# Three instructions' places in a four-layer graph kernel: a normalisation, a check of weights and a set of columns

## The reference

```python
h = relu(layernorm(x))
# layer 0: w = row softmax of adj^T where adj != 0 (adj is 0 or 1: a mean over neighbours)
x += BN(w^T @ BN(w @ h @ kernel_1 + bias_1) @ kernel_2 + bias_2)   # BN over all graphs and nodes
# layer 1 (A): Wh = h @ W^T; s, t = Wh @ a_src, Wh @ a_dst
x += softmax(where(adj, leaky_relu(s_i + t_j), -inf)) @ Wh
# layer 2 (B): e = leaky_relu(h_i * a_k . h_j), k picked by adj; adj == 1 is the only kind here
x += softmax(where(adj == 1, e, -9e15)) @ h
# layer 3 (C): as layer 1 with its own W and a, then elu
x += elu(softmax(where(adj > 0, leaky_relu(s1_i + s2_j), -9e15)) @ Wh)
```

## Time and profile before

| | us |
|---|---|
| median of three runs | 1505.93 |
| profiled execution | 1506.49 |
| its span (first to last instruction) | 1504.7 |
| TensorE busy | 1375.7 (91%) |
| VectorE busy | 1177.1 (78%) |
| ScalarE busy | 818.6 (54%) |
| GpSimd busy | 384.2 (26%) |

### The profile page before, as it was taken

One profiled execution on the slowest core, in us unless ns is written; L12 is line 12 of the kernel. 1 busy time (PEld: TensorE's weight loads), 2 busy tenths in 40 slices (PEclk: granted clock), 3 DMA queues, 4 the chain that ended last, 5 costly groups with the idle time before them and its releaser, 6 DMA issues.

```text
span 1504.7 us, 33033 instructions
## 1 busy us (share of the span) xinstructions
PE 1375.7 (91%) x12642; PEld 1238.7 (82%) x12642; DVE 1177.1 (78%) x3400; ACT 818.6 (54%) x1843; POOL 384.2 (26%) x337
## 2 busy tenths in 40 slices
PE   5899998899946888999999999999999999999886
PEld 5899997555536778999999999989999889999785
DVE  5788885788746668888888898888988889887565
ACT  4788885122243564565746656556565565654621
POOL 6343430000010304314133141331423314223020
PEclk9999998899968989999999999999999999999998
DMA  9999993566612213132331432314323134132111
GB/s 206 224 226 231 223 217 130 183 241 239 208 39 76 71 41 94 50 106 83 94 93 50 113 100 71 95 51 109 106 64 99 52 104 113 44 86 56 30 43 44
DMA packets 111840, 169.36 MB, mean 113 GB/s; under 512 B 9808, under 2 KB 61760, under 8 KB 109632
## 3 DMA queue, kind: packets, MB, share of 16 engines
q1 hardware_dynamic: 87264, 125.20, 28.9%
q0 software_dynamic: 19584, 33.56, 12.3%
q10 hardware_dynamic: 4832, 8.45, 1.5%
HBM read 158.74 MB, written 42.00 MB: 133 GB/s over the span
## 4 chain that ended last, share of the span: by engine, by line
PE 48%; DVE 11%; DVEq 4%; ACT 3%; POOL 2%; issue 2%; ACTq 0%
PE ps L1703 31%; PE ps L1662 3%; PE ps L1685 2%; PE ps L1716 2%; PE ps L1630 2%; DVE wts_C L1010 2%; PE ps L1674 2%; PE ps L1676 2%; PE ps L1675 2%; POOL wts_B L923 1%; DVEq L1033 1%; DVE xC L1087 1%; DVE st_B L945 1%; DVE xB L1040 1%; PE ps L1639 1%
## 5 line engine op out<-in xcount | busy, mean ns | idle before, releaser
L1703 PE MATMUL ps<-hV,wts_B 128*128 128x129 f32 x2048 | 252.4, 279 | 13.0 <-POOL wts_B L923 5.2
L923 POOL TENSOR_TENSOR wts_B<-wts_B,off 128x1024 f32<-128x1024 f32 (+7 forms) x128 | 177.8, 1413 | 323.0 <-PE ps L1685 323.0
L1703 PEld LDWEIGHTS ps<-hV,wts_B 128*128 128x128 f32 x2048 | 241.3, 194 | 17.4 <-POOL wts_B L923 7.3
L1703 PE MATMUL ps<-hP_A,wts_A 128*128 128x129 f32 x1920 | 230.9, 275 | 1.1 <-ACT xB L1429 0.7
L1703 PEld LDWEIGHTS ps<-hP_A,wts_A 128*128 128x128 f32 x1920 | 221.5, 191 | 3.8 <-DVE hP_C L994 2.9
L1703 PE MATMUL ps<-hP_C,wts_C 128*128 128x129 f32 x1920 | 220.1, 274 | 0.0
L1703 PEld LDWEIGHTS ps<-hP_C,wts_C 128*128 128x128 f32 x1920 | 217.4, 191 | 0.5
L1010 DVE SCALAR_TENSOR_TENSOR wts_A<-row_A,least_A,ring_A 128x1024 f32<-128x1024 f32 x128 | 161.0, 1274 | 11.4 <-ACT row_A L1384 7.9
L1010 DVE SCALAR_TENSOR_TENSOR wts_C<-row_C,least_C,ring_C 128x1024 f32<-128x1024 f32 x120 | 166.7, 1401 | 0.0
L316 ACT ACTIVATE maskT<-ps 128x1024 fp8e4<-128x1024 bf16 x128 | 131.2, 1025 | 45.4 <-PE ps L360 33.0
L372 PE MATMUL ps<-x,adj_b 128*128 128x129 f16 x896 | 121.3, 224 | 20.9 <-DVE x L237 13.9
(11 more groups left out here) (243 smaller groups left out, 2713.7 us busy)
## 6 DMA issues: line engine op xcount, KB each, us to landing
adj_b<-in_adj POOLq DMA_DIRECT2D x120, 256.0 KB, 10.4
maskT_scratch<-maskT SPq DMA_DIRECT2D x16, 1024.0 KB, 6.8
ring_A<-maskT_scratch SPq DMA_DIRECT2D x64, 256.0 KB, 3.1
off<-maskT_scratch SPq DMA_DIRECT2D x32, 512.0 KB, 6.6
ring_C<-maskT_scratch SPq DMA_DIRECT2D x64, 256.0 KB, 3.4
xa<-in_x SPq DMA_DIRECT2D x16, 512.0 KB, 16.3
whT_b<-whT_scratch SPq DMA_DIRECT2D x16, 512.0 KB, 4.8
pTf_scratch<-pT_b SPq DMA_DIRECT2D x16, 512.0 KB, 2.9
```

Of the source, the lines that this page charges most:

```text
L923: pool.tensor_tensor(w, w, off_fp8[:, k, k * P:N], ALU.mult).then_inc(S["B", "up"], 1)
L1703: last = nc.tensor.matmul(Q_SLOTS[c // 2 % 2][:, c % 2, 0:PW], wts[y][:, j, c * P:c * P + P], src[:, j, :], start=(j == 0), stop=(j == T - 1))
```

## The change

Three edits, none of which adds or removes an instruction.

1. In the first stage, shifts, normed, high and low of the next graph each move ahead by one tile: shifts from c = 3 to c = 2, low from c = 6 to c = 5. Statistics and moments stay at c = 0 and 1.
2. In the second stage, later_weights_dve moves behind graph(1) on VectorE, and later_weights_pe behind the first product on TensorE.
3. In the last stage, in steps with C at work, columns("A", i + 1) moves ahead of weights("C", i - 2, 4). exponents stays behind it. This is so in steps 2 to 14, 13 of them.

```diff
--- before.py
+++ after.py
@@ -261,13 +261,13 @@
                                 stats(b + 1, c)
                             if more and c == 1:
                                 moments(b + 1)
-                            if more and c == 3:
+                            if more and c == 2:
                                 shifts(b + 1)
-                            if more and 3 <= c < 5:
-                                normed(b + 1, c - 3)
+                            if more and 2 <= c < 4:
+                                normed(b + 1, c - 2)
+                            if more and c == 4:
+                                high(b + 1)
                             if more and c == 5:
-                                high(b + 1)
-                            if more and c == 6:
                                 low(b + 1)
                         rest(b, T - 1)
                         nc.vector.tensor_copy(rdeg_all[:, b * T:b * T + T], rdg[:, :])
@@ -644,8 +644,8 @@
 
                     first_norm_dve(dve)
                     graph(0, 0, True)
+                    graph(1, 1, True)
                     later_weights_dve(dve)
-                    graph(1, 1, True)
                     for k in range(0, B // 2 - 1):
                         for par in range(2):
                             stats(k * 2 + par, par)
@@ -726,9 +726,9 @@
                     first_norm_pe(pe)
                     pe.wait_ge(m_kept, 1)
                     rows(0, 0, 0, True)
-                    later_weights_pe(pe)
                     rows(1, 1, 0, False)
                     product(0, 0, True)
+                    later_weights_pe(pe)
                     rows(2, 0, 1, False)
                     product(1, 1, True)
                     rows(3, 1, 1, False)
@@ -1257,10 +1257,11 @@
                         if AA:
                             stats("B", newB, 1)
                             moments("B")
+                        if nextA and i != 0:
+                            columns("A", i + 1)
                         if CA:
                             weights("C", i - 2, 4)
                         if nextA and i != 0:
-                            columns("A", i + 1)
                             exponents("A", i + 1)
                         if AA:
                             shifts("B", i)
```

## The result

| | before | after |
|---|---|---|
| median, 7 runs each, one chip | 1506.73 us | 1515.8 us |
| lowest and highest | 1505.83, 1508.25 | 1512.51, 1519.18 |
| ratio, 95% interval | 1 | 1.0061 (1.005 to 1.0073) |
| profiled execution, its span | 1506.49, 1504.7 | 1515.19, 1513.4 |
| first stage, until the last rest (L251) starts | 249.32 | 269.33 |

The program is 0.6% slower, at the time that was predicted (1515.3). Two single runs of the experiments stand apart: one of the twelve of part 2 alone took 1516.61 us at a mean granted clock of 0.916 (the others 0.965 to 0.967) and is in its ratio, one of the six of parts 2 and 3 took 6394.82 us and is not.

A forecast was written before the change was run, and what follows sets the result against it. It took three nearly full engines to bound the first stage and TensorE's issue the last. 18.8 - 3.6 - 5.8 = +9.4 on a span of 1504.7 gave 1515.9 profiled, 1515.3 as median; whole range 1506 to 1526.

The forecast's parts named there:

- Part 1, +18.8: First stage: normalisation a tile earlier lengthens the batch period from 13.95 to 15.44 us; +18.8 us, bounds 13 to 23.
- the stall at tile 5: First stage, TensorE: tile 5's products wait something over 1 us for tile 2's rest, roughly replacing 0.93 us per batch.
- the dearer one: First stage: tile 6's tail falls behind low, so ScalarE's divide of tile 6 starts 1.82 us later.
- Part 2, -3.6: Second stage: the weights' check behind the first product lets rows(1) start 4.1 us earlier; -3.6 us, bounds -4.7 to -2.5.
- I let rows(1) and the product last as long as they do now: Second stage, TensorE: assumed unchanged durations for rows(1) and the first product, within the -3.6 us.
- Part 3, -5.8: Last stage: columns ahead of weights C 4 bring sf_B 0.53 us earlier in 11 steps; -5.8 us, bounds -6.8 to +4.8.
- The choice that L1010, begun 0.22 behind the power's start, leaves it alone: Last stage: GpSimd's power taken as free, 1.64 us instead of 2.60 to 2.63, with rs_B at 898.39.
- Power blocked later: Rival, last stage: the moved L1010 still stretches GpSimd's power, costing +4.8 us; total 1525.9 us, chance 0.19.
- Row_A takes the whole gain: Rival, last stage: sf_B stays where it is, so the columns' move gains 0; total 1521.1 us, chance 0.12.
- Exchange of waits in the first stage: Rival: TensorE's 0.93 us wait per batch becomes 1.2 to 1.3 at tile 5, +3.6 us; total 1500.1, chance 0.07.
- Full gain: Rival: the first stage's 13.9 us of TensorE waits for x go; total 1482.6 us, chance 0.02.
- The sum: Whole program: 18.8 - 3.6 - 5.8 = +9.4 us, giving 1515.3 us; chance 0.57.

The follow-up runs named there:

- part 2 alone: The kernel before with only the weights' check moved behind the first product in the second stage; ratio 0.9987 to the kernel before.
- parts 2 and 3: The kernel before with the check and the columns moved but the first stage's normalisation left where it was; ratio 0.9927 to the kernel before.
- after, rest 2 ahead: The kernel after with VectorE's rest of tile 2 put ahead of shifts, into the wait for the power; ratio 1.0035 to the kernel before.
- part 1 alone: The kernel before with only the first stage's normalisation moved a tile earlier; ratio 1.0129 to the kernel before.
- part 3 alone: The kernel before with only the columns moved ahead of weights C 4 in the last stage; ratio 0.996 to the kernel before.
- the loop without ScalarE's waits: The kernel before with check and columns moved, and ScalarE's store of the first half moved behind the next batch's first divide; ratio 0.9932 to the kernel before.

## Why the prediction was right, step by step

- **Part 1, +18.8: measured +19.4.** Its rows came as worked out: sf_a bound to the power with 1.17 us idle (forecast: 1.1 or more), low 5.13 behind sf_a, divide 6 at 6.75 (forecast 68.09 - 61.34 = 6.75), the last rest at 9.51 (9.49), 5.97 (5.95) from it to sf_a, period 15.45 in the regular batches and 15.53 in the mean (15.44).
- **One step of part 1 was wrong though the sum was right.** I wrote that the stall at tile 5 "would roughly replace the 0.93 us" and that tile 6 was "the dearer one". It is, but by 0.25 us only: with tile 6's tail back ahead of low the loop is still 15.21. The stall makes TensorE's transposes late for ScalarE, which has no slack left until the last rest, and so costs 1.25 us a batch by itself. I followed the late tile on TensorE only, not to the engine behind it.
- **Part 2, -3.6: -3.4 and some -5 in the runs (-2.0 with the run of 1516.61 us), -4.6 in the rows.** From the first row (L622) to the second people copy are 27.82 us before and 23.23 after. The mis-sized term is "I let rows(1) and the product last as long as they do now". From the end of L630 to the second L622 are 7.96 us before and 3.14 after, 4.8 less where I had 4.1. The granted clock tells why (last column but two). Windows of the kernel before, then of the kernel after:

```profile
270.00:274.00 4.00, 0.23 (x1) 0.24 (x2) 3.68 (x11) 1.04 (x1) 0.00 (x0) 0.50 0.54 229
274.00:278.00 4.00, 4.00 (x19) 3.86 (x20) 1.37 (x9) 0.00 (x0) 0.00 (x0) 0.50 0.00 0
```

```profile
288.00:289.00 1.00, 0.16 (x1) 0.19 (x2) 0.90 (x2) 0.27 (x1) 0.00 (x0) 1.00 1.06 438
289.00:290.00 1.00, 1.00 (x9) 1.00 (x9) 1.00 (x2) 0.78 (x1) 0.00 (x0) 0.86 0.99 418
290.00:291.00 1.00, 1.00 (x7) 1.00 (x7) 1.00 (x2) 0.00 (x0) 0.00 (x0) 0.50 0.88 369
```

  Before, TensorE had idled 7.29 us and the clock was 0.50, the 1.2 GHz level, while rows(1) ran: 3.76 us. After, it had idled 3.72; the clock was still full (2.4 GHz) when rows(1) began at 288.84 and was at 0.50 from 290 on: 2.95 us. The shorter wait alone doesn't give this. All four kernels with the wait of 7.29 us have 3.76, but the ten with part 2, all with a wait of 3.72 or 3.73, have anything from 2.02 at a clock of 1.00 (part 2 alone) to 3.75 at 0.50 (after, rest 2 ahead):

```profile
271.25 2.02 PE L710 MATMUL ps<-k,whT_b 128*128 128x128 f32 x16 [3.73 <-DVE row L630]
```

```profile
285.83 3.75 PE L712 MATMUL ps<-k,whT_b 128*128 128x128 f32 x16 [3.73 <-DVE row L632]
```

  The other 1.4 us of the stage (17.19 from the last rest to the first row, after 15.82) lie ahead of the edit, and 1.0 of them is the clock too: the 16 matmuls of rows(0) took 3.00 us at a granted clock of 0.64 before and 2.04 at 1.00 after. No part of the change brings it: from the last rest to the first row are 16.01 us with part 1 alone, 16.28 with part 2 alone, 17.28 with part 3 alone and 15.83 with parts 2 and 3. What decides the clock here stays open, as do the other 0.4 us.
- **Part 3, -5.8: measured -6.0.** Worked out per step 0.53, in the trace 0.54. The choice that L1010, begun 0.22 behind the power's start, leaves it alone was the dearest one (it decided on the rival of a power blocked later, 0.19), and it was right: 1.64 us. The rule of the Trainium skill (GPSIMD Engine Reference, Key points) that the two engines contend when VectorE reads two SBUF inputs holds here only when L1010 is running at the power's start: the power takes 2.60 to 2.63 us with L1010 begun 0.17 ahead, though they overlap for 1.11 us, and 1.64 with it begun 0.22 or 0.56 behind, though all of its 1.28 us lie over the power. L1010 itself takes 1.28 either way. And not every VectorE instruction does it: at the start of the power of 569.29, which takes 1.64, one of 0.82 us with an input in PSUM was running:

```profile
569.11 0.82 DVE L1025 TENSOR_TENSOR wts_B<-ps,off 128x640 f32<-128x640 f32 x1
```

- **The rivals.** Power blocked later: out; all 13 powers rs_B from 600.59 to 1339.40 take 1.64 us. The 14th, at 1398.23, in a step without columns, where L1010 begins 0.16 ahead of it, still takes 2.60. Row_A takes the whole gain: out; it starts 2.46 after sf_B, as before, and moved with it. Exchange of waits in the first stage (1500.1): out, the last rest moved by 1.84, not by less than 0.5. Full gain: out.
- **The sum** hit within 0.5 us, partly by luck: part 1 was 0.6 under its measure, part 2 a microsecond short on the other side. By stages the profiled executions differ by +20.0, -6.0 and -5.4 where the terms were +18.8, -3.6 and -5.8; about 1.8 of the -6.0 is a clock that no term held (1.0 at rows(0), 0.8 at rows(1)).

## What to carry to other kernels

Moving a step that waits for another engine ahead is worth nothing unless what it waits for moves too: it turns the work that used to cover the wait into work behind the block. Follow each displaced instruction to the engine that consumes it, and on through that engine's queue; where three engines are nearly full, several closed chains can be nearly as long (here 15.45 and 15.20 us), and an experiment that removes one shows only the next. And "idle time" on an in-order engine can be filled only by work whose own input is ready by then.

## What the hardware showed that I had not expected

- A GpSimd power of 128x8 was lengthened by 0.96 to 0.99 us (1.64 to 2.60 or 2.63) when VectorE's L1010 had started 0.17 us ahead of it, and not at all when the same 1.28 us instruction started 0.22 us behind it. 0.39 us in the start of one instruction decide over about a microsecond on another engine.
- The same 16 matmuls behind the same wait of 3.7 us took from 2.02 to 3.75 us in ten kernels, at a granted clock from 1.00 to 0.50; behind 7.3 us of waiting they took 3.76 in all four. A profile of one execution can so credit an edit with up to 1.7 us that are the clock's.
- In the first stage the DMA share is 1.07 before and 0.97 after; the same 512 KB of x land in a median of 16.3 us before and in 4.0 after. In the loop without ScalarE's waits, which stays at 13.91, VectorE waits for this load. That the adjacency's loads hold it back is the likely reading of that share; it wasn't tested.
